# Packed 64-row decay and fifth mixing products, a regrouped order of mixing steps, and the last channel addition on GpSimd

## The chip, the cores and the metric

The kernel runs on 1 core of one Trainium2 chip. The metric is the device time of one execution in microseconds (us); lower is better. All arithmetic is in fp32. In the profile PE is TensorE's matmul stream and PEld its weight loads, DVE is VectorE, ACT is ScalarE, POOL is GpSimd, and SP is SyncE, which issues the DMAs.

## What is computed

Two layers over x of 64 sequences, 64 steps, 256 channels. The first is a transformer layer: self attention, cross attention, and an MLP (not touched). The second is a recurrent block, of which this is the part that matters:

```python
xxx = jnp.tanh((xa + sx * maa_x) @ maa_w1).reshape(b, l, 5, 32)
xxx = jnp.einsum('blfd,fde->blfe', xxx, maa_w2)          # five mixing products
xm = xa[:, :, None] + sx[:, :, None] * (maa_stack + xxx) # xk, xw, xv, xr, xg
w = jnp.exp(-jnp.exp(time_decay + jnp.tanh(xw @ td_w1) @ td_w2))
r, k, v = xr @ Wr.T, xk @ Wk.T, xv @ Wv.T
g = silu(xg @ Wg.T)
# per head: out_t = r_t (u * k_t v_t + s);  s = k_t v_t + w_t * s   (a scan over the 64 steps)
x1 = x + groupnorm(out) * g @ Wo.T
xc = layernorm(x1)                                       # channel mixing
xk2, xr2 = xc + sx2 * ffn_maa_k, xc + sx2 * ffn_maa_r
return x1 + sigmoid(xr2 @ Wfr.T) * (square(relu(xk2 @ Wfk.T)) @ Wfv.T)
```

## The kernel before

x lives in SBUF as 32 tiles of 128 rows. The attention part works through all tiles twice and ends near 480 us. `late_phase` then works in 16 runs (`RUNS`) of 256 rows (`RT`, two tiles). It is written as one instruction stream per engine; each engine runs its stream strictly in order, and semaphores tie the streams together. So the order within a stream is the schedule. `body(s, u)` is a pipeline stage of every engine: in body s the scan of run s goes on together with the mixing and projections of run s + 1, the normalisation of run s + 2, the MLP of run s + 3, the group normalisation of run s - 1 and the output projection and residual of run s - 2. Bodies -2 to 3 are written out, 4 to 11 are a hardware loop, 12 to 15 are written out again.

Names that the change and the prediction's steps touch:

- **PE.** `mix_pair` (L1031) makes mixing products 0 to 3, in pairs, from 32-row tiles of weights; even-numbered steps go to PSUM bank `even` (bank 4) and odd ones to `odd` (bank 5). `mix_last` (L1042) makes the fifth product into `even` from a 128-row weight tile, half of whose rows are zero: `maa_w2b[:, c]` holds the real weights only in rows 64c onward (the other tile's 64 rows are zero), so the four 128x128 matmuls contract over 128 rows to use 64. `decay` (L1082) makes `td_w2` products into bank `small` (bank 3) in the same way. `project` (L1071, and L1052 for the decay's first product) makes the projections NW, NV, NK, NR, NG; `up` (L982) and `down` (L991) are the MLP; `sum_heads` (L1109) reduces the read states; `project_out` (L1142) is the output product of run s - 2. An fp32 matmul shows as two records, so "x8" is four matmuls.
- **DVE.** A run's scan is 8 groups. Group n is `key_values` (L1749), `scan` (L1763) and `read` (L1774; for groups 2 and 3 POOL reads, L901). Between the groups stand, by hand, `mix` (L1729, two halves a step), `add_heads` (L1791), `add_residual` (L1826, adds run s - 2's output product to x), `centre` (L1795, L1802), `sum_squares` (L1812), `mlp_residual` (L1697) and others. Steps 0 and 1 of `mix` stand after group 3's read, step 2 in n == 4, step 3 in n == 5, step 4 in n == 6.
- **POOL.** `mix` (L892) adds xa to each mixed product; step m is called at n = m + 3. `add_mlp_bias` (L868), `scale` (L909, group normalisation, after all groups), `step_back` (L875), `make_bonus` (L884).
- **ACT.** `decay` (L1425) takes the exponential of the decay products; `make_decays` (L1433) that of its negative, for the next run's scan.
- **Channel mixing.** Its 16 runs (`ch_` functions) start in the last three bodies (`early(s)`: s = 13, 14, 15, two runs a body) and go on alone after them. On DVE `ch_mix` (L1867) makes two inputs, `ch_finish` multiplies tanh + 1 by the value product (L1875) and then adds half of that to x (L1879). `ch_shift` (L938) is on POOL; `ch_transpose`, `ch_keys` (L1251), `ch_receptances` (L1266) and `ch_values` (L1281) on PE. In n == 2 of these bodies DVE's order is `add_heads`, `ch_mix` (which waits for POOL's `ch_shift`), `mlp_moments`, `add_residual`. PE's `mix_pair(s + 1, 0)` waits for `add_residual(s - 2)`, since `project_out` wrote bank `odd`:

```python
if m == 0:
    pe.wait_ge(mixer_tanh, r + 1)
    ...
    if later(r - 2):
        pe.wait_ge(x_ready, r - 2)
```

SP stores run s when `ch_out_ready` reaches s + 1.

## Time and profile before

| | |
|---|---|
| median of 3 runs | 1130.16 us (1126.83 to 1130.65) |
| the profiled execution | 1127.48 us, span 1125.7 us |
| mean granted TensorE clock | 0.988 |
| busy over the span | PE 95%, DVE 81%, ACT 63%, POOL 53% |
| attention part | to about 480 us |
| bodies of the late phase | 480 to 1050 us, one full one about 33.7 us |
| channel mixing alone | 1050 us to the end |

The span is that of the instructions on the core; 1.8 us of the execution's time lie around it. The median of the three runs is 2.7 us over the profiled execution. A share of the whole span says little here: the stages have different limits, so each is read by itself.

### The profile page before, as it was taken

How to read it: one execution, taken by the hardware profiler on the slowest of the kernel's cores; microseconds unless marked ns; L12 is line 12 of the kernel's file. 1: busy time of each engine (PE TensorE's matmuls, PEld its weight loads, DVE VectorE, ACT ScalarE, POOL GpSimd, SP SyncE). 2: the span in 40 equal slices, each digit the busy share in tenths (PEclk: the TensorE clock that was granted, in tenths of full speed). 3: DMA queues.
4: the chain of work that ended last, by engine and by line, in shares of the span. 5: the costliest groups of instructions: out<-in, count | busy, mean ns of one | idle time of the engine just before them, and what ended most of it. 6: DMA issues, size and time to landing. Idle time of an engine off the chain costs nothing.

```text
span 1125.7 us, 34405 instructions
## 1 busy us (share of the span) xinstructions
PE 1067.1 (95%) x12992; PEld 898.8 (80%) x12992; DVE 914.3 (81%) x1677; ACT 705.7 (63%) x1606; POOL 591.5 (53%) x520
## 2 busy tenths in 40 slices
PE   5899999999999998999999999999999997887798
PEld 4889889888988987778778888778888776665677
DVE  5987777888777775129999999999999999899864
ACT  4778788777877875555545565546555545535574
POOL 4787878878788784034443444443444343433121
PEclk9999999999999998999999999999999999889999
DMA  9500000011111110022233332133332123304011
GB/s 331 167 4 2 0 0 3 3 40 47 44 37 46 38 38 2 1 59 68 54 75 85 85 85 60 35 75 84 84 84 61 34 74 85 84 2 120 20 38 57
DMA packets 39868, 65.01 MB, mean 58 GB/s; under 512 B 4385, under 2 KB 26209, under 8 KB 39393
## 3 DMA queue, kind: packets, MB, share of 16 engines
q1 hardware_dynamic: 39776, 63.75, 21.3%
q8 instruction: 62, 1.02, 0.4%
q14 instruction: 30, 0.24, 0.1%
HBM read 55.35 MB, written 8.39 MB: 57 GB/s over the span
## 4 chain that ended last, share of the span: by engine, by line
PE 83%; DVE 9%; issue 4%; ACT 3%; POOL 1%; DMA 0%; DVEq 0%; ACTq 0%; POOLq 0%
PE psum L982 10%; PE psum L353 10%; PE psum L991 9%; PE psum L1071 9%; PE psum L267 5%; PE psum L336 5%; PE psum L368 5%; PE psum L297 4%; PE psum L280 3%; PE psum L1031 3%; PE psum L1109 2%; PE psum L1251 2%; PE psum L310 2%; PE psum L1142 2%; DVE shared L1763 2%
## 5 line engine op out<-in xcount | busy, mean ns | idle before, releaser
L1763 DVE TENSOR_TENSOR_SCAN shared<-late_wT,shared 128x512 f32<-128x512 f32 x128 | 175.6, 1372 | 0.0
L892 POOL TENSOR_TENSOR late_xm<-late_mixed,late_xa 128x512 f32<-128x512 f32 x64 | 91.4, 1438 | 106.2 <-DVE late_mixed L1729 106.1
L232 POOL TENSOR_TENSOR shared<-shared,att_row_max 128x512 f32<-128x512 f32 x128 | 132.5, 1054 | 17.3 <-DVE att_row_max L564 17.3
L353 PE MATMUL psum<-shared 128*128 128x128 f32 x1024 | 126.7, 277 | 0.0
L453 ACT ACTIVATE shared<-shared 128x512 f32<-128x512 f32 x128 | 80.5, 631 | 67.5 <-POOL shared L232 67.4
L982 PE MATMUL psum<-late_glnT,w 128*128 128x256 f32 x512 | 119.8, 387 | 1.8 <-ACT late_glnT L1359 1.8
L353 PEld LDWEIGHTS psum<-shared 128*128 128x128 f32 x1024 | 121.0, 194 | 0.2 <-ACT shared L462 0.2
L564 DVE TENSOR_REDUCE att_row_max<-shared 128x8 f32<-128x512 f32 x128 | 86.8, 679 | 41.0 <-POOL shared L225 40.9
L991 PE MATMUL psum<-w,late_hT 128*128 128x256 f32 x512 | 118.6, 380 | 1.0 <-ACT late_hT L1368 0.9
L901 POOL TENSOR_TENSOR shared<-shared,late_rT 128x512 f32<-128x512 f32 x32 | 40.8, 1274 | 143.0 <-DVE shared L1763 143.0
L982 PEld LDWEIGHTS psum<-late_glnT,w 128*128 128x128 f32 x512 | 95.8, 192 | 18.0 <-issue 2.8
L991 PEld LDWEIGHTS psum<-w,late_hT 128*128 128x128 f32 x512 | 93.6, 190 | 12.6 <-ACT late_hT L1368 1.8
L225 POOL TENSOR_TENSOR shared<-shared 128x512 f32<-128x512 f32 x64 | 80.1, 1273 | 39.8 <-DVE shared L557 38.2
L225 POOL TENSOR_TENSOR shared<-shared,self_bias 128x512 f32<-128x512 f32 x64 | 80.2, 1277 | 31.0 <-DVE shared L557 31.0
L1368 ACT ACTIVATE late_hT<-psum,cols 128x256 f32<-128x256 f32 x128 | 53.8, 471 | 65.7 <-PE psum L982 65.3
L1749 DVE TENSOR_TENSOR shared<-shared,psum 128x504 f32<-128x504 f32 x128 | 85.5, 669 | 11.2 <-ACT shared L1412 11.0
L267 PEld LDWEIGHTS psum<-shared 64*64 64x64 f32 x4096 | 66.3, 136 | 21.3 <-issue 21.2
L1729 DVE SCALAR_TENSOR_TENSOR late_mixed<-psum,cols,late_sx 128x256 f32<-128x256 f32 x160 | 67.9, 474 | 14.3 <-PE psum L1031 9.4
L462 ACT ACTIVATE shared<-psum 128x512 f32<-128x512 f32 x128 | 68.5, 586 | 9.1 <-PE psum L280 9.1
L267 PE MATMUL psum<-shared 64*64 64x17 f32 x4096 | 72.7, 209 | 0.0
L336 PE MATMUL psum<-shared 128*128 128x128 f32 x512 | 69.5, 280 | 1.5 <-issue 1.5
L424 ACT ACTIVATE shared<-psum,cols 128x256 f32<-128x256 f32 x128 | 65.4, 565 | 8.1 <-PE psum L310 5.3
(167 smaller groups left out, 2433.7 us busy)
## 6 DMA issues: line engine op xcount, KB each, us to landing
shared<-v_rows SPq DMA_DIRECT2D x64, 512.0 KB, 7.3
shared<-in_enc SPq DMA_DIRECT2D x64, 128.0 KB, 2.6
v_rows<-shared SPq DMA_DIRECT2D x64, 64.0 KB, 1.8
out<-x SPq DMA_DIRECT2D x16, 256.0 KB, 2.0
x<-in_x SPq DMA_DIRECT2D x7, 512.0 KB, 9.8
w<-in_w SPq DMA_DIRECT2D x2, 1024.0 KB, 17.3
shared<-in_cross_mask SPq DMA_DIRECT2D x1, 1024.0 KB, 12.3
shared<-in_w_qkv SPq DMA_DIRECT2D x1, 768.0 KB, 4.8
```

What stands on the lines that cost most here:

```text
L225: nc.gpsimd.tensor_tensor(zs, zs, bias.unsqueeze(1).to_broadcast([P, PAIRS, S]), ALU.add).then_inc(biased, 1)
L232: nc.gpsimd.tensor_tensor(zs, zs, peak.unsqueeze(2).to_broadcast([P, PAIRS, S]), ALU.subtract).then_inc(shifted, 1)
L267: last = nc.tensor.matmul(out_banks[e ^ b][rows, pair * 32:pair * 32 + HD + 1], zT[keys, pair, rows], values[keys, u, e ^ b, pair, :], sta ...
L336: last = nc.tensor.matmul(vv[:, e * P:(e + 1) * P].rearrange("p (r d) -> p r d", d=HD), KV[k][:, u % 2, kb, e * S:e * S + P], wv[:, kb, v0 ...
L353: last = nc.tensor.matmul(dst[:, half * P:(half + 1) * P], w[:, kb, c0 + half * P:c0 + (half + 1) * P], src[:, u % 2, kb, 0:P], start=(kb ...
L564: nc.vector.tensor_reduce(out=row_max[:, u % 2, half * PAIRS:(half + 1) * PAIRS], in_=z[:, u % 2, half, :].rearrange("p (h k) -> p h k", k=S),
L892: nc.gpsimd.tensor_tensor(xm[m % XM].rearrange("p h (b t) -> p (h b) t", t=S), mixed[:, m % 2, :, :].rearrange("p h (b t) -> p (h b) t", t=S),
L982: last = nc.tensor.matmul(bank[:, (h % 2) * RT:(h % 2 + 1) * RT], w["w1"][:, kb, h * P:(h + 1) * P], glnT[:, kb, :], start=(kb == 0), stop ...
L991: last = nc.tensor.matmul(mlp[:, c * C:(c + 1) * C], hT[:, h, c * P:(c + 1) * P], w["w2"][:, h, :], start=(h == 0), stop=(h == HIDDEN - 1))
L1071: last = nc.tensor.matmul(bank[:, half * RT:(half + 1) * RT], w[name][:, kb, half * P:(half + 1) * P], xm[m % XM][:, kb, :], start=(kb == ...
L1749: nc.vector.tensor_tensor(st[:, n, :, :, 1:S], v_rep[:, n // PER_SUM, n % PER_SUM * JG:(n % PER_SUM + 1) * JG, :].rearrange("p j (b t) -> ...
L1763: nc.vector.tensor_tensor_scan(states, wT[:, u, half, :, :, :].rearrange("p j b t -> p (j b t)"), states, 0.0, ALU.mult, ALU.add).then_inc ...
```

## The change

It has four parts.

1. `decay` and `mix_last` on PE contract over 64 rows: each of the two tiles c uses its own row half (rows 64c to 64c + 63) of weights and input, and the two write different banks. The decay products now lie in `small` (c = 0) and in the upper half of `odd` (c = 1); the fifth mixing product lies in the lower halves of `even` and `odd`. ACT's `decay` and DVE's `mix(4)` read them with patterns over two banks.
2. Since `odd` holds mixing product 3 until DVE has read it, PE's `mix_last` waits for `mix(3)` instead of `mix(2)`, and `decay` stands behind `mix_last` instead of ahead of `down(s + 3, 0)`. DVE's `mix(3)` stands right behind `mix(2)` in n == 4, `mix(4)` moves from n == 6 to n == 5, and `mix(4)` waits for ACT's `decay` as well.
3. The addition to x of channel mixing moves from DVE (L1879) to POOL (`ch_add`) for 15 of 16 runs; the factor 0.5 moves into ACT's `Square` (scale sqrt(0.5) on its input).
4. In the last three bodies `add_residual(s - 2)` stands ahead of `ch_mix` in n == 2.

```diff
@@ -737,6 +737,8 @@
 
         small, even, odd, proj, o_bank, mlp = (core.banks[i] for i in (3, 4, 5, 2, 0, 1))
         k_bank, r_bank = core.banks[6:8]
+        decays = core.psum[:, 3 * 512:3 * 512 + 2 * 1280].rearrange("p (c n) -> p c n", c=CH)[:, :, 0:RT]
+        fifth = core.psum[:, 4 * 512:6 * 512].rearrange("p (c n) -> p c n", c=CH)[:, :, 0:RT]
 
         ch_xn = core.shared[:, 8192:9216].rearrange("p (a b c) -> p a b c", b=2, c=256)
         ch_xc = core.shared[:, 9216:10256].rearrange("p (a b c d) -> p a b c d", b=2, c=4, d=65)
@@ -915,6 +917,8 @@
                     step_back(s + 1)
                 if there(s):
                     make_bonus(s, u)
+                if early(s - 1):
+                    ch_add(early_run(s - 1, 1), 1)
                 for n in range(GROUPS_R):
                     if n == 5 and there(s + 3):
                         add_mlp_bias(s + 3)
@@ -926,6 +930,8 @@
                         mix(s + 1, n - 3)
                     if n == 3 and early(s):
                         ch_shift(early_run(s, 1), 1)
+                    if n == 6 and early(s):
+                        ch_add(early_run(s, 0), 0)
                 if there(s - 1) and not s_is(s, RUNS - 1):
                     scale(s - 1)
                 if s_is(s, RUNS - 1):
@@ -940,18 +946,29 @@
                                         ch_xc[:, u, :, :, 1:S + 1].rearrange("p h b t -> p (h b) t"),
                                         ALU.subtract).then_inc(ch_sx_ready, 1)
 
+            def ch_add(r, u):
+                pool.wait_ge(ch_rv_ready, r + 1)
+                xs = core.x[:, ds(r, CH * C)]
+                nc.gpsimd.tensor_tensor(xs, ch_rr[:, u, :], xs, ALU.add).then_inc(ch_out_ready, 1)
+
             def channel(s, u):
                 if there(s + 2):
                     ch_shift(s + 2, u)
+                if there(s + 1):
+                    ch_add(s, u)
 
             add_mlp_bias(0)
             bodies(pool, body)
             ch_shift(EARLY + 1, 1)
+            ch_add(EARLY - 1, 1)
             ch_shift(EARLY + 2, 0)
             scale(RUNS - 2)
             scale(RUNS - 1)
+            ch_add(EARLY, 0)
             ch_shift(EARLY + 3, 1)
+            ch_add(EARLY + 1, 1)
             ch_shift(EARLY + 4, 0)
+            ch_add(EARLY + 2, 0)
             channel(EARLY + 3, 1)
             channel_runs(pool, channel)
 
@@ -1035,12 +1052,13 @@
                             last.then_inc(mix_ready, 1)
 
             def mix_last(r):
-                pe.wait_ge(mixed_ready, r * NMIX + NMIX - 2)
-                for half in range(HALVES):
-                    for c in range(CH):
-                        a = half * RT + c * P
-                        last = nc.tensor.matmul(even[:, a:a + P], core.maa_w2b[:, c, half * P:(half + 1) * P],
-                                                mixer_b[:, :], start=True, stop=True)
+                pe.wait_ge(mixed_ready, r * NMIX + NMIX - 1)
+                for half in range(HALVES):
+                    for c, bank in enumerate((even, odd)):
+                        rows = slice(c * DD, (c + 1) * DD)
+                        last = nc.tensor.matmul(bank[:, half * P:(half + 1) * P],
+                                                core.maa_w2b[rows, c, half * P:(half + 1) * P],
+                                                mixer_b[rows, :], start=True, stop=True)
                 last.then_inc(mix_ready, 1)
 
             def project(r, m):
@@ -1077,10 +1095,11 @@
                 if later(r - 1):
                     pe.wait_ge(centred_ready, r - 1)
                 for half in range(HALVES):
-                    for c in range(CH):
-                        a = half * RT + c * P
-                        last = nc.tensor.matmul(small[:, a:a + P], core.td_w2[:, c, half * P:(half + 1) * P],
-                                                decay_in[:, :], start=True, stop=True)
+                    for c, bank in enumerate((small, odd)):
+                        rows = slice(c * DD, (c + 1) * DD)
+                        a = c * RT + half * P
+                        last = nc.tensor.matmul(bank[:, a:a + P], core.td_w2[rows, c, half * P:(half + 1) * P],
+                                                decay_in[rows, :], start=True, stop=True)
                 last.then_inc(decay_ready, 1)
 
             def bonus_sums(r):
@@ -1190,11 +1209,11 @@
                     ch_receptances(early_run(s, 0), 0)
                 if mixing:
                     project(s + 1, NV)
-                    decay(s + 1)
                 if mlp_run:
                     down(s + 3, 0)
                 if mixing:
                     mix_last(s + 1)
+                    decay(s + 1)
                 if early(s):
                     ch_values(early_run(s, 0), 0)
                 if mlp_run:
@@ -1422,9 +1441,9 @@
             def decay(r):
                 act.wait_ge(decay_ready, r + 1)
                 for half in range(HALVES):
-                    last = nc.scalar.activation(decay_exp[:, half * RB:(half + 1) * RB, :].rearrange("p b t -> p (b t)"),
-                                                small[:, half * RT:(half + 1) * RT], ACT.Exp,
-                                                bias=col(core, "time_decay", half))
+                    last = nc.scalar.activation(
+                        decay_exp[:, half * RB:(half + 1) * RB, :].rearrange("p (c b) t -> p c (b t)", c=CH),
+                        decays[:, :, half * P:(half + 1) * P], ACT.Exp, bias=col(core, "time_decay", half))
                 last.then_inc(decay_expd, 1)
 
             def make_decays(r, u):
@@ -1524,7 +1543,7 @@
                     act.wait_ge(up_ready, RUNS * UPS)
                 if later(r - 1):
                     act.wait_ge(ch_value_ready, r - 1)
-                nc.scalar.activation(ch_kk[:, u, :], ch_relu[:, :], ACT.Square).then_inc(ch_kk_ready, 1)
+                nc.scalar.activation(ch_kk[:, u, :], ch_relu[:, :], ACT.Square, scale=0.5 ** 0.5).then_inc(ch_kk_ready, 1)
 
             def ch_tanh(r, u):
                 act.wait_ge(ch_recept_ready, r + 1)
@@ -1725,11 +1744,17 @@
                 dve.wait_ge(mix_ready, r * NMIX + m + 1)
                 if later(r) or m >= 2:
                     dve.wait_ge(xm_ready, r * NMIX + m - 1)
-                for half in range(HALVES):
+                if m == NMIX - 1:
+                    dve.wait_ge(decay_expd, r + 1)
+                for half in range(HALVES):
+                    if m == NMIX - 1:
+                        products = fifth[:, :, half * P:(half + 1) * P]
+                    else:
+                        products = (even, odd)[m % 2][:, half * RT:(half + 1) * RT].rearrange("p (c t) -> p c t", c=CH)
                     last = nc.vector.scalar_tensor_tensor(
-                        out=mixed[:, m % 2, half, :], in0=(even, odd)[m % 2][:, half * RT:(half + 1) * RT],
+                        out=mixed[:, m % 2, half, :].rearrange("p (c t) -> p c t", c=CH), in0=products,
                         scalar=col(core, "maa_stack", MIX[m] * HALVES + half),
-                        in1=sx[:, half, :, :].rearrange("p b t -> p (b t)"), op0=ALU.add, op1=ALU.mult)
+                        in1=sx[:, half, :, :].rearrange("p (c b) t -> p c (b t)", c=CH), op0=ALU.add, op1=ALU.mult)
                 last.then_inc(mixed_ready, 1)
 
             def gate(r, u):
@@ -1874,10 +1899,11 @@
                 dve.wait_ge(ch_rr_ready, r + 1)
                 nc.vector.scalar_tensor_tensor(out=ch_rr[:, u, :], in0=ch_rr[:, u, :], scalar=1.0, in1=ch_bank("value", r),
                                                op0=ALU.add, op1=ALU.mult).then_inc(ch_rv_ready, 1)
-                dve.wait_ge(ch_rv_ready, r + 1)
-                xs = core.x[:, ds(r, CH * C)]
-                nc.vector.scalar_tensor_tensor(out=xs, in0=ch_rr[:, u, :], scalar=0.5, in1=xs, op0=ALU.mult,
-                                               op1=ALU.add).then_inc(ch_out_ready, 1)
+                if r == RUNS - 1:
+                    dve.wait_ge(ch_rv_ready, r + 1)
+                    dve.wait_ge(ch_out_ready, r)
+                    xs = core.x[:, ds(r, CH * C)]
+                    nc.vector.tensor_tensor(xs, ch_rr[:, u, :], xs, ALU.add).then_inc(ch_out_ready, 1)
 
             def channel(s, u):
                 ch_finish(s - 1, 1 - u)
@@ -1915,10 +1941,11 @@
                         add_heads(s - 1, 1 - u)
                     if n == 2:
                         if early(s):
+                            add_residual(s - 2)
                             ch_mix(early_run(s, 0), 0)
                         if there(s + 2) and not s_is(s, -2):
                             mlp_moments(s + 2)
-                        if there(s - 2):
+                        if there(s - 2) and not early(s):
                             add_residual(s - 2)
                     if n == 3 and there(s + 1):
                         mix(s + 1, 0)
@@ -1932,17 +1959,16 @@
                             centre(s - 1, 1 - u)
                         if there(s + 1):
                             mix(s + 1, 2)
+                            mix(s + 1, 3)
                         if early(s):
                             ch_mix(early_run(s, 1), 1)
                     if n == 5:
-                        if there(s + 1):
-                            mix(s + 1, 3)
                         if early(s):
                             ch_finish(early_run(s, 0), 0)
                         if there(s - 1) and not s_is(s, RUNS - 1):
                             sum_squares(s - 1)
-                    if n == 6 and there(s + 1):
-                        mix(s + 1, 4)
+                        if there(s + 1):
+                            mix(s + 1, 4)
                     if n == 7 and s_is(s, RUNS - 1):
                         ch_mix(EARLY, 0)
```

## Rows read from the trace of the kernel before

**Rows 1.** Busy time by stretch: us, then PE, PEld, DVE, ACT, POOL busy (instructions), clock, DMA.

```profile
506.50:536.70 30.20, 30.20 (x177) 24.59 (x176) 27.09 (x43) 16.83 (x37) 14.60 (x11) 1.00 0.34 80
...
770.87:804.59 33.72, 33.72 (x210) 27.32 (x209) 32.11 (x52) 18.93 (x42) 14.76 (x12) 1.00 0.30 70
...
939.46:981.00 41.54, 32.04 (x185) 24.35 (x184) 38.13 (x62) 19.54 (x45) 16.07 (x13) 0.92 0.27 63
...
1050.00:1126.00 76.00, 65.74 (x334) 55.70 (x332) 46.37 (x97) 45.27 (x92) 12.22 (x11) 1.00 0.10 39
```

**Rows 2.** The chain that ended last, one loop body: start us, us, what.

```profile
615.20 1.06 PE psum L1031 x8
...
621.37 0.62 PE psum L1052 x8
...
622.99 1.92 PE psum L1071 x8
624.91 0.89 PE psum L1082 x8
...
627.53 0.89 PE psum L1042 x8
...
631.88 1.73 PE psum L1071 x8
```

**Rows 3.** Timeline of another loop body: start us, us, instruction, [idle before, releaser].

```profile
787.96 2.00 DVE L1763 TENSOR_TENSOR_SCAN shared<-late_wT,shared 128x512 f32<-128x512 f32 x1
788.83 2.20 POOL L868 TENSOR_TENSOR x<-x,rows 128x512 f32 x1
...
791.98 0.87 DVE L1729 SCALAR_TENSOR_TENSOR late_mixed<-psum,cols,late_sx 128x256 f32<-128x256 f32 x2
...
792.77 0.67 DVE L1749 TENSOR_TENSOR shared<-shared,psum 128x504 f32<-128x504 f32 x1
792.93 1.20 POOL L892 TENSOR_TENSOR shared<-late_mixed,late_xa 128x512 f32<-128x512 f32 x1 [1.91 <-DVE late_mixed L1729]
...
793.36 1.85 DVE L1763 TENSOR_TENSOR_SCAN shared<-late_wT,shared 128x512 f32<-128x512 f32 x1
...
795.72 0.84 ACT L1425 ACTIVATE late_decay_exp<-psum,cols 128x256 f32<-128x256 f32 x2
...
796.80 1.19 POOL L892 TENSOR_TENSOR late_xm<-late_mixed,late_xa 128x512 f32<-128x512 f32 x1 [2.67 <-DVE late_mixed L1729]
...
798.20 1.22 DVE L1763 TENSOR_TENSOR_SCAN shared<-late_wT,shared 128x512 f32<-128x512 f32 x1
...
801.01 2.03 POOL L892 TENSOR_TENSOR late_xm<-late_mixed,late_xa 128x512 f32<-128x512 f32 x1 [3.03 <-DVE late_mixed L1729]
...
803.00 1.10 POOL L909 TENSOR_TENSOR shared<-shared,late_rstd 128x512 f32<-128x512 f32 x1
...
803.13 0.68 DVE L1749 TENSOR_TENSOR shared<-shared,psum 128x504 f32<-128x504 f32 x1 [0.34 <-ACT shared L1412]
...
804.59 0.69 DVE L1697 TENSOR_TENSOR x<-psum,x 128x512 f32 x1 [0.78 <-PE psum L991]
```

**Rows 4.** Timeline of body 13, the first with channel mixing.

```profile
951.09 1.26 POOL L901 TENSOR_TENSOR shared<-shared,late_rT 128x512 f32<-128x512 f32 x1 [2.88 <-DVE shared L1763]
951.51 2.31 DVE L1867 SCALAR_TENSOR_TENSOR late_hT<-shared,cols 128x256 f32<-128x256 f32 x4
...
954.98 0.69 DVE L1826 TENSOR_TENSOR x<-psum,x 128x512 f32<-128x512 f32 x1
...
955.81 1.95 PE L1031 MATMUL psum<-late_mixer_a,maa_w2a 32*128 32x256 f32 x8 [4.96 <-DVE x L1826]
...
973.26 0.69 DVE L1875 SCALAR_TENSOR_TENSOR w<-w,psum 128x512 f32<-128x512 f32 x1 [2.14 <-PE psum L1281]
...
973.98 0.69 DVE L1879 SCALAR_TENSOR_TENSOR x<-w,x 128x512 f32<-128x512 f32 x1
```

**Rows 5.** Busy time by stretch of 2 us within body 13, columns as in rows 1.

```profile
956.00:958.00 2.00, 2.00 (x10) 1.30 (x9) 1.66 (x3) 0.00 (x0) 0.54 (x1) 0.50 0.00 0
```

## The prediction

> **What bounds the kernel now.** I read the busy time by stretch first [rows 1]. In a full loop body (33.72 us) PE is busy for all of it and DVE for 32.11 us: PE sets the period, and DVE is close behind. Body 13 is another case: 41.54 us, PE busy for 32.04, DVE for 38.13, and the granted clock averages 0.92. In body 0 (506.50 to 536.70) PE is full and DVE has 3 us left. After 1050 us PE is busy 65.74 of 76 us and DVE 46.37. The chain that ended last is PE alone through the loop bodies. So each part has to be costed where it falls: PE's time counts in the loop as long as DVE does not take over; DVE's time counts in the last three bodies.
>
> How near DVE is, the timeline shows: in one body it waits 0.34 us for k's copy and 0.78 us for the MLP [rows 3]; with the small gaps that those waits cover, it could start `mlp_residual` 1.28 us earlier (`read(7)` starts at about 802.10, two steps of 0.61 us later comes 803.31, against 804.59). That 1.28 us is all the cover that DVE's new waits have.
>
> **PE: two products at half height.** `decay` and `mix_last` take 0.89 us each [rows 2], 8 records at 0.11. The 32-row tiles of `mix_pair` run in pairs on two row groups: 8 records with 256 columns take 1.06 us, where 8 full ones take 1.73 [rows 2]. Of the 1.06, 4 x 0.216 = 0.86 is streaming and 0.20 is the change of tile shape; the full product behind tiles pays 0.19 too (1.92 against 1.73 [rows 2]). The 64-row case with 128 columns is not in the trace; nearest is L1052, 8 tiled records with 128 columns in 0.62. By that pattern both products need 8 pairs x 0.108 = 0.86, plus 0.20 going in and 0.19 coming out, as they now stand together: 1.25 against 1.78, so 0.53 us less per body. Bounds: if pairs didn't overlap at all, 1.78 + 0.39, a loss of 0.39; with no cost for the changes of shape, a gain of 0.92. I take 0.53 by the 32-row rows, since they use row groups and two banks in the same way. PE alone would then have a period of 33.2 us.
>
> The Trainium skill (TensorEngine Tiling, Key Properties) says that a change of tiling mode drains the array. The 0.19 to 0.20 us in the rows agree; a rule of "up to 2x" without it would give 0.89.
>
> **PE's new waits.** `mix_last` now needs `mix(3)`. DVE would end it about 1.6 us after 791.98 [rows 3], at 793.6; PE comes to it at about 795.0, behind `down(s + 3, 0)`. Hidden, with 1.4 us of cover. `decay` ends about 2 us later than before, near 796.2 (795.0 + 1.25), so ACT starts L1425 near 796.3 instead of 795.72 [rows 3] and ends at 797.2. Behind it wait `make_decays` (needed only in the next body) and the normalisation of run s + 2, which has some 0.7 us of cover: nothing. The ACT form over two banks has the same count of elements: no cost, between -0.1 and +0.1.
>
> **DVE and POOL: the order of the mixing steps.** No DVE instruction is added, so its own work stays at 32.4 us. But scans and POOL's operations on SBUF exclude each other. `scan(5)` is issued at 793.36 under POOL's `mix(2)` (792.93, 1.20) and takes 1.85 instead of 1.22; POOL's `mix(4)`, issued at 801.01 just behind `scan(7)`, takes 2.03; and L868, issued at 788.83 while a scan from 787.96 was already waiting, let that scan go first [rows 3]. So: whoever asked first. POOL's `mix(3)` and `scan(6)` are apart now (796.80, 798.20: 1.19 and 1.22 [rows 3]). After the change, counted from `mix(2)`'s start M = 791.98:
> - `mix(3)` ends at M + 1.6, `key_values(6)` runs to M + 2.2, and only then does `scan(5)` ask. POOL's `mix(2)` runs from M + 0.95 to M + 2.15 and its `mix(3)` is ready behind it, so POOL goes on first, narrowly, to M + 3.27. `scan(5)` ends at M + 4.4. Before, it ended at M + 3.23 but with `mix(3)` (0.79) still to do: a loss of 0.4.
> - `sum_squares`, then `mix(4)` from M + 6.0 to M + 6.9 (`decay`'s exponential is there at M + 5.2, no wait); POOL's `mix(4)` runs M + 6.95 to M + 8.14; `scan(6)`, issued at M + 7.38, waits 0.7.
> - `scale` (1.10 us, L909 [rows 3]) now comes behind `mix(4)`, lets `scan(6)` go first and holds up `scan(7)` by 0.45 (before, it ran at 803.00 beside no scan).
> - What `mix(4)` itself held up is POOL's, not DVE's. Rounding taken in, `read(7)` is 1.3 us later than before.
>
> The cover is 1.28. DVE's period becomes 33.7 us: it takes over exactly where PE was, and PE's 0.53 us is not seen in bodies 2 to 12. Bounds of the port waits: none of them gives 32.45 (PE's 33.2 binds); each of the three operations holding up a scan for its whole length (1.2 + 1.2 + 1.1 against 0.7 now) gives +2.8, less 1.28: +1.5 per body.
>
> **Bodies -1, 0 and 1.** DVE has more than 1.3 us left, so PE's gain counts: 3 x 0.53 = 1.6 us.
>
> **Bodies 13 to 15.** In body 13 `ch_mix` is issued at 951.51 but POOL's L901 holds SBUF until 952.35; then it takes its four steps, and `add_residual` comes at 954.98. PE waits 4.96 us for it, and its next product runs at 0.50 of the clock: 1.95 us for 8 records instead of 1.13 [rows 4, 5]. So `add_residual` (0.69) fits into the hole ahead of `ch_mix`: free, and PE starts `mix_pair` 3.5 us earlier, at the full clock (the 2.4 GHz level). DVE then loses two small waits for `mix_pair` and, above all, the 2.14 us ahead of `ch_finish` [rows 4]. Moving L1879 away saves 0.61 from start to start, twice a body. Against that: POOL's additions (1.26 us, the price of L901, same shape [rows 4]; nothing to 2.0 if a scan is in front) hold up `scan(1)` after the first `ch_finish` by 0.65, so there nothing is won; the other lies beside `sum_squares` and `mix(4)`. The regrouped mixing costs its 1.3 again, partly within these waits, and part of `ch_mix` of the second run meets POOL's `mix(3)`. Sum: body 13 -2.3, body 14 (the same three waits stand there again, at 994 to 1015 us) -2.1, body 15, with no mixing, about 0: -4.4 us. Bounds: DVE's gaps of 3.4 and 3.8 us and six L1879 all gone, -10.9; the port taking nearly all, -1.
>
> **After 1050 us.** PE is the bound (keys, values, receptance, transposition: 5.6 us a run against DVE's 3). POOL is busy 12 of 76 us [rows 1] and takes nine more additions of 1.3 us beside idle time; the order ch_shift, ch_add puts each addition some 2 us ahead of the next shift's data. The last run's addition stays on DVE, and the store behind it too. The factor in `Square` is free. 0, between -1 and +1.
>
> The Trainium skill (GPSIMD Engine Reference, Engine selection) advises against additions on GpSimd, as about twice as slow: 1.26 against 0.69 us agrees. By it alone the tail would lose if POOL were on its chain; there it is idle for 64 of 76 us [rows 1].
>
> **Sum.** 1127.5 - 1.6 - 0 - 4.4 = 1121.5 us on the profiled execution, which ran 2.7 us under the median of the three runs; the same -6.0 on the median is 1124.2. I give **1123**, 1.5 over the sum, half the distance to the median; the rivals' times have the same 1.5. About 0.5% (5.6 us) is what a measurement of this kernel can tell from no change, so the forecast lies just at that line.
>
> **Rivals.**
> - *The scan goes first (0.25).* POOL's lead at M + 2.15 is under 0.1 us. If `scan(5)` gets in ahead of `mix(3)`, it ends 0.7 us earlier than now, `mix(4)` waits some 0.25 for the exponential, the rest is as above: DVE's period 33.0, PE's 33.2 binds, and 11 bodies give another 5.8: 1121.5 - 5.8 + 1.5 = 1117.
> - *The port takes more than the cover (0.15): slower.* Place: `scan(5)`, `scan(6)`, `scan(7)` of bodies 2 to 14. It decides once their waits together pass the present ones by more than 1.28 + 0.5 us a body. With half the upper bound, 0.75 x 11 = 8.3, and bodies 13 and 14 winning 1.5 less: 1121.5 + 9.8 + 1.5 = 1132.8. For it: three POOL operations are moved next to scans; against: the rows show turns being taken. The Trainium skill (SBUF — State Buffer, two separate sides) has the pair of ports as an exclusive lock, held for the whole instruction by whoever starts first. By it the cost of each meeting is what is left of the operation, as counted.
> - *The tiles don't overlap (0.07).* PE's period rises by 0.39: 14 x 0.39 - 4.4 on the profiled execution gives 1128.6 + 1.5 = 1130. It would contradict the 32-row rows.
> - *The clock falls all the same (0.08).* PE now runs ahead in bodies 13 and 14 and waits about 3 us ahead of the second key product. If the clock falls there, half of the 4.4 is lost: 1125.
>
> **Range and chances.** The forecast (0.45) by itself holds 1119 to 1127. 1113 to 1132 takes in the second case and most of the third. Faster by over 0.5%: half of the forecast and the first rival, 0.48; slower by over 0.5%: part of the port case, 0.12; within: 0.40.
>
> **What would show it.** The chain in the loop turns from PE to DVE, the period stays within 0.1 of 33.7 (33.2 for the first rival, above 34.1 for the second). L1082 and L1042 together take 1.25 us. `scan(5)` takes 2.2 us, `scan(6)` 1.9. PE's 4.96 us is gone and the clock is 1.00 in bodies 13 and 14. If the periods of bodies 13 and 14 don't fall by about 2 us each, the forecast is wrong in its main term.

## The result, and the profile after

The changed kernel takes **1120.26 us** (median of 4 runs, 1118.13 to 1122.14), and the kernel before 1130.22 us on the same chip: ratio 0.9918 (0.9889 to 0.9947), 9.3 us less by the ratio and 10.0 between the two medians. A second series gave 1118.04 us and 0.9911 (0.9889 to 0.9932), by the ratio 10.0 us less. Gains below are by the ratio. The forecast was 1123 us. The profiled execution took 1118.86 us, 8.6 less than that of before.

The page of the changed kernel, busy time and the chain that ended last by engine, and below them the chain of the kernel before:

```profile
PE 1061.3 (95%) x12992; PEld 883.5 (79%) x12992; DVE 916.1 (82%) x1662; ACT 702.6 (63%) x1606; POOL 608.1 (54%) x535
PE 60%; DVE 27%; issue 7%; ACT 3%; DVEq 1%; DMA 1%; SPq 0%; POOL 0%; ACTq 0%; POOLq 0%
...
PE 83%; DVE 9%; issue 4%; ACT 3%; POOL 1%; DMA 0%; DVEq 0%; ACTq 0%; POOLq 0%
```

The first line hardly differs from that of before. The chain does: DVE's share went from 9% to 27% of the span, and in the loop bodies the chain now runs through DVE's instructions. The busy time by stretch of the changed kernel (columns as in [rows 1]; one full body stands for the loop, the fourth and fifth stretch begin inside bodies 14 and 15):

```profile
505.97:535.64 29.67, 29.67 (x177) 23.69 (x176) 27.41 (x43) 16.80 (x37) 13.67 (x11) 1.00 0.34 78
768.04:801.49 33.45, 33.41 (x209) 26.27 (x208) 32.95 (x52) 18.69 (x42) 14.80 (x12) 1.00 0.31 72
936.73:977.26 40.53, 31.49 (x200) 23.76 (x199) 39.25 (x64) 20.89 (x47) 15.75 (x14) 1.00 0.33 77
977.26:1014.00 36.74, 30.88 (x187) 23.62 (x186) 35.34 (x54) 18.00 (x39) 17.60 (x14) 0.95 0.27 63
1014.00:1041.00 27.00, 22.47 (x123) 16.82 (x122) 26.33 (x36) 12.54 (x28) 11.24 (x8) 0.94 0.15 53
1041.00:1117.00 76.00, 66.94 (x332) 56.41 (x330) 38.52 (x87) 45.24 (x92) 24.59 (x21) 0.97 0.10 39
```

Body 0 took 30.18 us before; the loop body took 33.72. In body 13 PE is busy for less time than before, at a clock of 1.00 instead of 0.92.

**Where the 8.6 us lie** in the two profiled executions, counted between starts of `mlp_residual` and, in the last bodies, of DVE's gate product:

| stretch | before | after | difference | predicted |
|---|---|---|---|---|
| up to body 0 | 506.51 | 505.97 | -0.54 | -0.53 |
| bodies 0 and 1 | 61.78 | 60.91 | -0.87 | -1.06 |
| bodies 2 to 11 | 337.37 | 335.11 | -2.26 | 0 |
| body 12 | 33.80 | 34.74 | **+0.94** | 0 |
| start of body 13 to body 14's gate | 51.48 | 47.53 | -3.95 | -2.3 |
| body 14's gate to body 15's | 39.26 | 36.66 | -2.60 | -2.1 |
| from there to the end | 95.5 | 96.2 | +0.7 | 0 |

The start of body 0 by itself says little: over the kernels of this study, whose attention part is the same, it lay anywhere between 503.40 and 507.15 us. Body -1 can be told apart, though: counted between starts of `mlp_residual` it took 26.59 us in the four traces with products at full height (before, e1, e2, e4) and 26.09 us in the ten with tiles. So 0.50 of the first row's 0.54 us is the tiles'.

The rows of bodies 12 and 13 have to be read together. The start of `mlp_residual` is a marker on DVE, and DVE comes to it later now in body 13, but has less to do behind it. The timeline of the kernel before, then that of the changed one, at the start of body 13:

```profile
940.65 1.89 DVE L1763 TENSOR_TENSOR_SCAN shared<-late_wT,shared 128x512 f32<-128x512 f32 x1
942.47 1.19 DVE L1855 SCALAR_TENSOR_TENSOR neg_mean<-neg_mean,rstd 128x20 f32<-128x20 f32 x1
...
937.92 1.22 DVE L1788 TENSOR_TENSOR_SCAN shared<-late_wT,shared 128x512 f32<-128x512 f32 x1
939.05 0.16 DVE L1880 SCALAR_TENSOR_TENSOR neg_mean<-neg_mean,rstd 128x20 f32<-128x20 f32 x1
```

From the start of `mlp_residual` to DVE's gate product body 13 takes 8.55 us before and 7.26 after. From gate product to gate product body 12 takes 35.02 us before and 34.76 after, and body 13 takes 42.93 and 40.27. So body 12 lost nothing, and bodies 12 and 13 together gave 3.0 us (0.94 against 3.95 in the table).

**In the loop**, the timeline of the changed kernel, DVE's and POOL's work around the moved mixing steps, one body:

```profile
789.11 1.65 DVE L1754 SCALAR_TENSOR_TENSOR late_mixed<-psum,cols,late_sx 128x256 f32<-128x256 f32 x4
790.05 1.19 POOL L894 TENSOR_TENSOR shared<-late_mixed,late_xa 128x512 f32<-128x512 f32 x1 [1.90 <-DVE late_mixed L1754]
791.19 1.18 POOL L894 TENSOR_TENSOR late_xm<-late_mixed,late_xa 128x512 f32<-128x512 f32 x1
791.26 2.20 DVE L1788 TENSOR_TENSOR_SCAN shared<-late_wT,shared 128x512 f32<-128x512 f32 x1
793.50 0.84 ACT L1444 ACTIVATE late_decay_exp<-psum,cols 128x256 f32<-128x256 f32 x2 [0.73 <-PE psum L1101]
795.06 0.88 DVE L1754 SCALAR_TENSOR_TENSOR late_mixed<-psum,cols,late_sx 128x256 f32<-128x256 f32 x2
796.02 1.18 POOL L894 TENSOR_TENSOR late_xm<-late_mixed,late_xa 128x512 f32<-128x512 f32 x1 [3.65 <-DVE late_mixed L1754]
796.43 1.85 DVE L1788 TENSOR_TENSOR_SCAN shared<-late_wT,shared 128x512 f32<-128x512 f32 x1
797.16 2.02 POOL L911 TENSOR_TENSOR shared<-shared,late_rstd 128x512 f32<-128x512 f32 x1
798.92 1.34 DVE L1788 TENSOR_TENSOR_SCAN shared<-late_wT,shared 128x512 f32<-128x512 f32 x1
```

`scan(5)` starts in the record 0.07 us after POOL's `mix(3)`, and POOL went first: the scan takes 2.20 us instead of 1.22. `scan(6)` takes 1.85, behind POOL's `mix(4)`. `scan(7)` is held for only 0.12 us (1.34) by `scale`. ACT's exponential is done at 794.34, DVE comes to `mix(4)` at 795.06: no wait. The chain of waits of the changed kernel over the same stretch (start, us, what) lies on these very instructions:

```profile
789.11 1.65 DVE late_mixed L1754 x4
790.76 0.59 DVE shared L1774
791.34 2.12 DVE shared L1788
...
795.06 0.88 DVE late_mixed L1754 x2
...
796.53 1.77 DVE shared L1788
```

**In the last bodies**, the timeline of the changed kernel, PE's products behind waits, and the first addition on POOL with the scan beside it:

```profile
948.94 1.13 PE L1048 MATMUL psum<-late_mixer_a,maa_w2a 32*128 32x256 f32 x8 [0.91 <-ACT late_mixer_b L1421]
967.43 1.97 PE L1270 MATMUL psum<-late_hT,WfkT 128*128 128x256 f32 x8 [2.92 <-DVE w L1900]
981.26 1.28 POOL L952 TENSOR_TENSOR x<-w,x 128x512 f32<-128x512 f32 x1 [1.95 <-DVE w L1900]
981.70 1.93 DVE L1788 TENSOR_TENSOR_SCAN shared<-late_wT,shared 128x512 f32<-128x512 f32 x1
988.60 1.13 PE L1048 MATMUL psum<-late_mixer_a,maa_w2a 32*128 32x256 f32 x8 [1.42 <-DVE x L1851]
1006.12 3.44 PE L1270 MATMUL psum<-late_hT,WfkT 128*128 128x256 f32 x8 [2.93 <-DVE w L1900]
1026.80 3.68 PE L1270 MATMUL psum<-late_hT,WfkT 128*128 128x256 f32 x8 [1.58 <-DVE late_hT L1892]
```

The wait of 4.96 us [rows 4] is down to 0.91, and `mix_pair` takes 1.13 us, not 1.95. A new wait of 2.9 us stands ahead of the second key product, and behind it the same eight records take 1.97 us in body 13 and 3.44 us in body 14.

### The profile page after: what moved, and what is told of

Same layout as the page of the kernel before. It is cut to its first block, busy times and chain, and to the rows that moved or that the text cites. A ratio compares the mean times of both kernels' runs of the same rounds, so it can differ in the third digit from the quotient of the medians.

```text
span 1117.1 us, 34410 instructions
## 1 busy us (share of the span) xinstructions
PE 1061.3 (95%) x12992; PEld 883.5 (79%) x12992; DVE 916.1 (82%) x1662; ACT 702.6 (63%) x1606; POOL 608.1 (54%) x535
## 4 chain that ended last, share of the span: by engine, by line
PE 60%; DVE 27%; issue 7%; ACT 3%; DVEq 1%; DMA 1%; SPq 0%; POOL 0%; ACTq 0%; POOLq 0%
PE psum L353 9%; DVE shared L1788 9%; PE psum L267 5%; PE psum L999 5%; PE psum L336 5%; PE psum L1008 4%; PE psum L368 4%; PE psum L1089 4%; DVE shared L1774 4%; PE psum L297 4%; PE psum L280 3%; DVE late_mixed L1754 3%; PE psum L1270 2%; PE psum L310 2%; PE psum L1300 2%
## 5 line engine op out<-in xcount | busy, mean ns | idle before, releaser
L1788 DVE TENSOR_TENSOR_SCAN shared<-late_wT,shared 128x512 f32<-128x512 f32 x128 | 192.4, 1503 | 0.0
L894 POOL TENSOR_TENSOR late_xm<-late_mixed,late_xa 128x512 f32<-128x512 f32 x64 | 79.7, 1255 | 59.9 <-DVE late_mixed L1754 56.3
```

Source lines behind the costliest of these rows:

```text
L1788: nc.vector.tensor_tensor_scan(states, wT[:, u, half, :, :, :].rearrange("p j b t -> p (j b t)"), states, 0.0, ALU.mult, ALU.add).then_inc ...
```

## The experiments

The ratio is always to the kernel before, which ran on the same chip in the same series, with its 95% interval. **Theory A** was the prediction's account; each rival stands in the text on record.

### The three parts, one at a time

**e1: the kernel before with the residual ahead of channel mixing alone.**

```diff
                         if early(s):
+                            add_residual(s - 2)
                             ch_mix(early_run(s, 0), 0)
...
-                        if there(s - 2):
+                        if there(s - 2) and not early(s):
                             add_residual(s - 2)
```

> The kernel before with the fourth part alone: add_residual ahead of ch_mix in bodies 13 to 15. Theory A (the hole in front of mix_pair and the half clock behind it are most of the gain of the last bodies): PE's waits of 4.96 and 3.66 us fall to about 1 us, body 13 gets about 2.5 us shorter and body 14 about 1.5, and the whole 3 to 5 us. The loop stays at 33.72 us a body. Theory B (DVE's own load is what bounds those bodies, and PE's hole only stands beside it): under 1.5 us.

1122.41 us, ratio 0.9962 (0.9944 to 0.998): -4.3 us. The loop body stays at 33.72 to 33.75. Gate to gate, body 13 takes 39.58 us (42.93 before) and body 14 37.28 (39.26). The timeline of this kernel has the short wait, and a product close to its full-clock length behind it, in both bodies:

```profile
949.95 1.13 PE L1031 MATMUL psum<-late_mixer_a,maa_w2a 32*128 32x256 f32 x8 [1.51 <-DVE x L1826]
989.53 1.18 PE L1031 MATMUL psum<-late_mixer_a,maa_w2a 32*128 32x256 f32 x8 [1.43 <-DVE x L1826]
```

So one moved call of 0.69 us is worth 4.3 us. Two things in this trace say how. In body 14 the clock is at 0.50 again right behind the product (from 991 to 997 us, for as long as before), and the body is 1.98 us shorter all the same: there the gain is not the clock's. And the call is nearly free on DVE: `ch_mix`, which now starts behind it, takes 1.73 us instead of 2.31 [rows 4], since POOL's L901 is all but over by then (it ends at 949.98, `ch_mix` starts at 949.72).

**e2: the kernel before with the additions on POOL alone** (the lines of part 3 of the change: `ch_add` on POOL, the factor in `Square`).

> The kernel before with the third part alone: the channel addition on GpSimd for 15 runs, factor in Square. Theory A (the second ch_finish of a body lies on DVE's path, but its addition then holds up scan(1) at the port): 0.6 us in each of bodies 13 to 15 at most, 0 to 2 us in all; scan(1) of bodies 14 and 15 takes 1.9 us instead of 1.22. Theory B (DVE's time in these bodies is worth its full price): six times 0.61 = 3.7 us. Neither expects anything of the part after the last body, where PE is the bound.

1127.98 us, ratio 0.999 (0.9973 to 1.0007): no difference that can be told from zero (-1.1 us by the ratio, +0.5 between the medians). The timeline of this kernel, body 14:

```profile
988.08 1.28 POOL L950 TENSOR_TENSOR x<-w,x 128x512 f32<-128x512 f32 x1 [1.95 <-DVE w L1890]
988.52 1.93 DVE L1778 TENSOR_TENSOR_SCAN shared<-late_wT,shared 128x512 f32<-128x512 f32 x1
```

DVE saves a step of 0.61 us and gets back a scan that is 0.71 longer (1.93 for 1.22). Body 13 takes 43.27 us, 0.34 more than before, body 14 38.64, 0.62 less.

**e3: the kernel before with the tiles and the new mixing order alone** (parts 1 and 2).

> The kernel before with the first two parts alone: 64-row tiles, decay behind mix_last, the regrouped mixing steps, mix(4) waiting for the exponential. Channel addition and residual as before. Theory A (PE's 0.53 us a body is gained, DVE's port waits take half of it back): loop body 33.5 us, 3 to 4 us by body 12, then the last bodies lose about 1 us to the port: 2 to 4 us faster in all. Theory B (the regrouping is only there to make room, the last bodies are where the change works): within 1 us of the kernel before.

1124.22 us, ratio 0.9971 (0.9954 to 0.9987): -3.3 us. Loop bodies take 33.43 to 33.58, body 12 34.74, and bodies 13 and 14 keep their holes (PE waits 4.10 and 3.67 us). The three parts sum to -4.3 - 1.1 - 3.3 = -8.7 us by the ratios, and to -7.7 by the medians, since e2's share is not distinct from zero; the whole gave -9.3 and -10.0. So they add up within what these series can tell.

### What holds the loop at 33.5 us

**e4: the changed kernel, both products at full height again, order kept.**

```diff
-                                                core.maa_w2b[rows, c, half * P:(half + 1) * P],
-                                                mixer_b[rows, :], start=True, stop=True)
+                                                core.maa_w2b[:, c, half * P:(half + 1) * P],
+                                                mixer_b[:, :], start=True, stop=True)
...
```

> The changed kernel with its matmuls of mix_last and decay at 128 rows again (zero rows of the weights back in), everything else as changed, the order and the two banks too. Theory A (tiles are worth 0.53 us of PE a body, DVE with its port waits needs 33.5): PE needs 33.7 and binds again, loop body 33.7 to 33.8 instead of 33.5, and the whole 3 to 5 us slower than the changed kernel. Theory B (DVE alone sets the loop body since the regrouping): no difference, loop body 33.5. If DVE's and PE's loads add up where both are full, it may be more than 33.8.

1122.84 us, ratio 0.996 (0.9942 to 0.9977), some 5 us slower than the changed kernel. Two starts of `mlp_residual` on its timeline, one body apart:

```profile
737.77 0.69 DVE L1716 TENSOR_TENSOR x<-psum,x 128x512 f32 x1
771.51 0.69 DVE L1716 TENSOR_TENSOR x<-psum,x 128x512 f32 x1
```

33.74 us: PE binds again at its old period, and the chain of this loop body is PE's alone. So DVE, with all of the port's waits, stays under 33.74, and the tiles do bring the 0.2 to 0.3 us a body that are seen.

**e5: the changed kernel with `centre` behind `mix(3)`.** Then POOL's `mix(2)` and `mix(3)` are over before DVE asks for `scan(5)`.

```diff
                     if n == 4:
-                        if there(s - 1) and not s_is(s, RUNS - 1):
-                            centre(s - 1, 1 - u)
                         if there(s + 1):
                             mix(s + 1, 2)
                             mix(s + 1, 3)
+                        if there(s - 1) and not s_is(s, RUNS - 1):
+                            centre(s - 1, 1 - u)
```

> The changed kernel with centre moved from ahead of mix(2) to behind mix(3) in n == 4, so that 1.4 us of DVE's work without the shared port stands between mix(3) and scan(5). Port theory (DVE binds the loop body at 33.5 us, of which scan(5) waits 1.0 us behind POOL's mix(3)): scan(5) falls from 2.2 to about 1.3 us, DVE's need drops under PE's 33.2, and the loop body becomes 33.2: 3 us less in all. Rival (33.5 is PE's own period with the tiles, or is set by the new wait of mix(4) for the exponential): the body stays at 33.5.

1116.53 us, ratio **0.9898** (0.9882 to 0.9915), the fastest kernel of the study. Loop bodies take 33.01 to 33.51, mostly 33.2. The timeline of this kernel:

```profile
789.72 1.22 DVE L1788 TENSOR_TENSOR_SCAN shared<-late_wT,shared 128x512 f32<-128x512 f32 x1
792.98 0.88 DVE L1754 SCALAR_TENSOR_TENSOR late_mixed<-psum,cols,late_sx 128x256 f32<-128x256 f32 x2 [0.37 <-ACT late_decay_exp L1444]
```

and its chain of waits, a little earlier in the same body:

```profile
790.86 0.65 PE psum L1059 x8
791.50 0.45 PE psum L1101 x8
791.95 3.65 PE psum L1008 x16
```

The scan is back at 1.22 us, `mix(4)` now waits 0.37 for the exponential, and the chain is PE's: this is what the first rival forecast, reached by another order. It also gives the tiles' price on the path, 0.65 + 0.45, and 0.19 for the product behind them: 1.29 us.

**e9: the changed kernel with `sum_squares` behind `mix(4)`**, so that POOL's `mix(4)` is over before `scan(6)`.

```diff
-                        if there(s - 1) and not s_is(s, RUNS - 1):
-                            sum_squares(s - 1)
                         if there(s + 1):
                             mix(s + 1, 4)
+                        if there(s - 1) and not s_is(s, RUNS - 1):
+                            sum_squares(s - 1)
```

> The changed kernel with sum_squares moved behind mix(4) in n == 5, so that POOL's mix(4) runs beside it instead of in front of scan(6). Port theory: scan(6) falls from 1.85 to 1.22 us; mix(4) then comes 1 us earlier and may wait 0.2 to 0.4 us for ACT's exponential; loop body 33.2 to 33.3. Rival (the wait for the exponential counts): mix(4) waits 0.5 us or more and the body stays at 33.5 or goes up.

1119.72 us, ratio 0.9935 (0.9919 to 0.9952), loop 33.46 to 33.54 (the last body 33.26): no gain over the changed kernel. Its timeline:

```profile
791.81 0.88 DVE L1754 SCALAR_TENSOR_TENSOR late_mixed<-psum,cols,late_sx 128x256 f32<-128x256 f32 x2 [0.19 <-ACT late_decay_exp L1444]
793.74 0.35 ACT L1490 ACTIVATE late_log_var<-late_moments,eps 128x66 f32<-128x66 f32 x1 [0.89 <-issue]
794.16 1.22 DVE L1788 TENSOR_TENSOR_SCAN shared<-late_wT,shared 128x512 f32<-128x512 f32 x1
794.30 1.59 PEld L1089 LDWEIGHTS psum<-shared,WkT 128*128 128x128 f32 x8 [0.26 <-DVE shared L1774]
796.19 0.42 PEld L1020 LDWEIGHTS psum<-ident,late_xn 128*128 128x128 f32 x4 [0.30 <-ACT late_xn L1400]
```

`scan(6)` did fall to 1.22 us, and `mix(4)` waits 0.19 us, both as the port theory expected; the loop body stayed at 33.5, as the rival expected, but not for the rival's reason. The chain of this body is PE's. ACT's `late_log_var` starts 0.08 us behind the end of the later `sum_squares`, the normalisation behind it in ACT's stream comes later, and PE's transposition of its result takes 0.55 us in the chain instead of e5's 0.44. The other half comes straight from DVE: the weight load of the key projection waits for `key_values`, and the projection takes 1.85 us in the chain instead of e5's 1.73. Together 0.23 us: 33.2 became 33.5. The wait went off the port and onto PE, by two ways that no expectation had.

**e7: both moves (e5 and e9) together.**

> Both moves of the last two together. Port theory: both scans at 1.22, PE binds at 33.2 us a body (PE's own sum: 33.73 less 0.53), no better than either alone if each already lets PE bind; 3 to 4 us less than the changed kernel. Rival (something besides the port keeps DVE at 33.5): as the changed kernel.

1117.93 us, ratio 0.9912 (0.9897 to 0.9927), loop 33.49 to 33.58. Both scans take 1.22 us, but `mix(4)` comes so early that it waits 1.30 us for the exponential:

```profile
794.40 0.88 DVE L1754 SCALAR_TENSOR_TENSOR late_mixed<-psum,cols,late_sx 128x256 f32<-128x256 f32 x2 [1.30 <-ACT late_decay_exp L1444]
```

The chain is PE's, with the same two products drawn out as in e9 (1.95 and 0.55 us). The expected 33.2 did not come.

### The last bodies

**e8: the changed kernel with the additions back on DVE** (part 3 undone).

> The changed kernel with the channel addition on DVE again, and the factor 0.5 in it. Theory A (the third part gives little, since each POOL addition ahead of scan(1) blocks it for 0.65 us): body 14 and 15 within 0.7 us each of the changed kernel, 0 to 2 us slower in all. Theory B (with the hole in front of mix_pair gone DVE alone bounds bodies 13 to 15, so that the addition is worth its price there): 0.6 us twice a body, 3 to 4 us slower.

1118.8 us, ratio 0.9916 (0.9895 to 0.9937), against 0.9918 and 0.9911 for the changed kernel. With e2, part 3 shows nothing that these series can tell from zero, in either surrounding. One thing in the trace of its profiled execution (1121.98 us) bears on part 4: the residual stands ahead of `ch_mix` here, PE waits only 1.43 us ahead of `mix_pair` in body 14, and the clock is at 0.50 from 991 to 1000 us all the same. That body takes 39.15 us gate to gate, where the changed kernel's takes 36.66. e4's profiled execution has the same (0.50 from 996 to 1005 us, 39.19).

**e6: the changed kernel with the residual back behind channel mixing** (part 4 undone; the diff of e1 the other way round).

> The changed kernel with add_residual behind ch_mix and mlp_moments again in bodies 13 to 15. Theory A (what the residual alone gave on the kernel before, 4.3 us, is lost): PE's hole ahead of mix_pair is 3.5 to 5 us again in bodies 13 and 14, and the kernel is 3 to 5 us slower than the changed one. Theory B (DVE, now fuller from the regrouping, bounds these bodies whatever PE does): within 2 us of the changed kernel.

1124.68 us, ratio 0.9968 (0.9954 to 0.9983): about 6 us slower than the changed kernel. The timeline of this kernel has the holes again, in bodies 13 and 14:

```profile
952.58 1.13 PE L1048 MATMUL psum<-late_mixer_a,maa_w2a 32*128 32x256 f32 x8 [4.10 <-DVE x L1851]
993.75 1.29 PE L1048 MATMUL psum<-late_mixer_a,maa_w2a 32*128 32x256 f32 x8 [3.65 <-DVE x L1851]
```

From 994 to 1002 us its granted clock averages 0.57, where the changed kernel's is 1.00.

**e10: the changed kernel with the first run's `ch_finish` right behind the second run's `ch_mix`**, to shorten the new wait of 2.9 us ahead of the keys.

```diff
                             ch_mix(early_run(s, 1), 1)
-                    if n == 5:
-                        if early(s):
                             ch_finish(early_run(s, 0), 0)
+                    if n == 5:
```

> The changed kernel with ch_finish of a body's first run right behind ch_mix of its second, at the end of n == 4, instead of behind read(5). The value product is there by then, and DVE's load is the same; only PE's wait ahead of the second key product shrinks, from 2.9 us to under 1. Clock theory (that wait is what lets the clock fall in bodies 13 and 14, and 3.44 us for eight records instead of 1.97 lies on the path): no stretch at half clock at that product, bodies 13 and 14 up to 1.5 us shorter in some executions, and the times of the runs less scattered; 1 to 4 us in all. Rival (these bodies are DVE's whatever the clock does): under 1 us.

1126.99 us, ratio 0.999 (0.9972 to 1.0009): 8 to 9 us **slower** than the changed kernel, all of its gain gone. The timeline of this kernel, body 14:

```profile
1003.91 0.69 DVE L1900 SCALAR_TENSOR_TENSOR w<-w,psum 128x512 f32<-128x512 f32 x1 [0.98 <-PE psum L1300]
1004.67 1.26 POOL L952 TENSOR_TENSOR x<-w,x 128x512 f32<-128x512 f32 x1 [2.82 <-DVE w L1900]
1005.10 1.93 DVE L1788 TENSOR_TENSOR_SCAN shared<-late_wT,shared 128x512 f32<-128x512 f32 x1
1010.20 3.65 PE L1089 MATMUL psum<-shared,WkT 128*128 128x256 f32 x8 [3.49 <-DVE shared L1774]
```

The wait ahead of the keys is short now (0.87), but DVE waits 0.98 us for the values, the addition on POOL then falls on `scan(5)`, and everything behind is later, until PE waits 3.49 us one product further on and runs at half clock after it. Two of these effects had not been counted, so the run is no clean test of the clock. Its profiled execution took 1122.40 us, 3.5 over the changed kernel's, and bodies 13 and 14 (41.49 and 39.00 us gate to gate, against 40.27 and 36.66) hold that; the median of its 12 runs is 4.6 us above that again; seven of them had a mean clock of 0.985 or less, and the one at 0.992 took 1120.45 us. How those divide between order and clock was not settled.

**e11: e5's and e10's edits together.**

> The changed kernel with centre behind mix(3) and ch_finish of the first run right behind ch_mix of the second. If the two gains are independent (port in the loop, PE's hole in the last bodies): loop body 33.2 us, and the whole 3 to 6 us under the changed kernel, the fastest of all so far. Rival: the last bodies give back what the loop gains, as the fastest so far.

1121.82 us, ratio 0.9949 (0.9931 to 0.9966): the loop runs at 33.22 to 33.25, and the last bodies give back more than it gains, with the same wait of 3.49 us ahead of the key projection.

### The same kernel again

**e12: the changed kernel, unaltered.**

> The changed kernel itself once more, with more runs, since its ratio of 0.9918 rests on four runs and its executions differ by 4 us. If the experiments add up (undoing the residual or the tiles costs 4 to 6 us, moving centre gains 2): ratio 0.990 to 0.993. If it comes out above 0.995, the losses of e4, e6 and e10 against it are smaller than they look and lie within the scatter of the last bodies' clock.

Median 1118.04 us, but the execution that was profiled took 1121.33, at a mean clock of 0.986 against 0.989. The timeline of that execution has the wait that stands at 967.43 in the first one, and another end:

```profile
968.07 3.75 PE L1270 MATMUL psum<-late_hT,WfkT 128*128 128x256 f32 x8 [2.93 <-DVE w L1900]
```

2.93 us of waiting, then 3.75 us for what took 1.97. Body 13 lasted 42.08 us gate to gate here, at a clock of 0.50 from 968 to 974 us, and 40.27 there. What one execution loses in this place is the size of the differences between parts of the change, so a statement on the last bodies needs the medians.

## Why the prediction was right, and where its sizes were off

The forecast's sign, range and mechanism held; the gain was 9.3 us instead of 6 to 7. In the two profiled executions it was 8.6 against a sum of 6.0, and nearly all of the difference is one term: bodies 2 to 11, counted at nothing, gave 2.26. Step by step:

- **The tiles: right.** 1.25 us predicted, 1.29 measured (e5), 0.49 us saved of 0.53. The change of shape costs 0.65 - 0.45 = 0.20 going in and 0.19 coming out. The third rival (no overlap) is out. The Trainium skill (TensorEngine Tiling, Key Properties) says that a change of tiling mode drains the array; the rows agree, and a plain halving would have promised 0.89.
- **PE's and ACT's new waits: right**, as long as the order is that of the change. `mix_last` and `mix(4)` wait for nothing. e7 shows how near the exponential was: with `mix(4)` some 2 us earlier it costs 1.30.
- **The port: right in kind, off by 0.2 us in size.** `scan(5)` 2.20 (2.2 predicted) and `scan(6)` 1.85 (1.9). The largest error is in the step that "`scale` ... holds up `scan(7)` by 0.45": it held it 0.12. `scale`, released at 798.28 by `scan(6)`, was done 0.90 us later and not 1.10, so only 0.26 us of it were left when `scan(7)` was requested at 798.92. The three losses were counted as 0.4, 0.7 and 0.45, which is 1.55 us, and were then taken as 1.3 without a working; with 1.55 the sum would have given a DVE period of 34.0. Measured they are 0.35, 0.63 and 0.12, or 1.10 (`read(7)` is 1.08 us later than before, counted from `mix(2)`), against a cover of 1.28. So DVE's period is 33.5 and not 33.7, and PE's gain was half seen where it was counted at zero: -2.26 us in bodies 2 to 11. e4 shows that without the tiles these bodies are back at 33.74, e5 that without the turn lost in `scan(5)` they are at 33.2. The first rival's condition was not met (POOL went first, by 0.07 us), though its size, 33.2 a body, was what e5 then gave. The second rival is out: the meetings take less than the cover. The Trainium skill (SBUF — State Buffer, two separate sides) gives the pair of ports to one engine for a whole instruction; the 2.20, 1.85 and 1.93 us are each what was left of POOL's operation (1.11, 0.77, 0.84) and then 1.08 or 1.09 us, which agrees.
- **Bodies -1, 0, 1: right** in the first two (-0.50 and -0.52 of -0.53 each), and -0.36 in body 1, at whose end DVE's wait of 0.86 us for the MLP is used up: -1.4 of -1.6 in all.
- **Body 12: right.** It was counted with the loop, at nothing. The 0.94 us in the table is the marker's: from gate product to gate product it went from 35.02 to 34.76 us.
- **Bodies 13 and 14: right in cause; the size of body 13 is open.** The forecast's main term was -2.3 and -2.1. The first profiled execution gave -2.7 and -2.6 from gate to gate, e12's, of the same kernel, -0.9 and -2.7: body 13 was 1.8 us longer at half clock. e1 has -3.35 and -1.98 from the residual alone. The charge that "the regrouped mixing costs its 1.3 again" was too high: in e3, where the regrouping stands without the residual, it moved these bodies by -0.17 and +0.42. The prediction names its terms here but doesn't add them up, so the rest can't be put down to one of them.
- **The clock: half right.** In the changed kernel's two executions it no longer falls at 956 and 996 us. But part 4 doesn't secure that: with it, the clock fell near the second of these places in e1, e4 and e8. The fourth rival had its place right too: behind the new wait of 2.9 us ahead of the keys it fell in body 14 (1006.12) and, in e12, in body 13 too. It took not "half of the 4.4": bodies 12 to 14 gave 5.6 us in the first execution and 3.9 in e12's. The +0.7 us of the tail goes with the clock as well, though no run separates the two: it took 95.5 us in the two executions whose clock stayed at 1.00 there (before and e3) and 96.2 in this one, with two stretches at 0.50 (1027 to 1030 us, 1054.5 to 1057.5).
- **Part 3: right, at nothing.** The addition holds up `scan(1)` (1.93 us) as predicted, and it brings DVE nothing on the path.

The forecast's time leaned 1.5 us towards the median of three runs; the before kernel's medians in the four series that followed were 1127.4 to 1128.0 us. So it leaned on scatter: against the median of 1120.26 the sum of 1121.5 would have missed by 1.2 us instead of 2.7. Profiled execution against profiled execution that sum missed by 2.6 (1118.86).

Three things are open. The gain of part 4 body by body can't be separated from the clock's scatter by single executions. In the direct comparison of e5 and the changed kernel the loop bodies differ by 0.2 to 0.3 us in the traces, but the intervals (0.9882 to 0.9915 and 0.9889 to 0.9932) overlap. And the share of the clock in e10 is not known.

## What to carry to other kernels

When two engines are near each other (here 33.7 and 32.4 us a body), taking 0.5 us a body from the one on the chain is worth only what the other leaves: make the sum for both. And when bodies are compared, count from a second marker too: one body seemed 0.94 us longer from one instruction and 0.26 shorter from another. A step of 0.7 us that makes another engine wait 5 us is worth more than its length (here 4.3 us for two of them): look in the trace for the longest waits of the bound engine and move up what ends them. And where two engines hold each other up at SBUF, put independent work between the requests; here POOL's operation went first by 0.07 us and a scan took 2.20 us, and with 1.4 us of other work in between it took 1.22 (e5).

## What the runs showed that was not expected

- **The same wait, two outcomes.** PE's wait of 2.92 to 2.93 us ahead of the keys was followed by the 2.4 GHz level in one execution (1.97 us for eight records) and by the 1.2 GHz level in another of the same kernel (3.75 us). A wait of 1.58 us was followed by 3.68 us for the same records (at 1026.80). In e1 and e8 the clock was at 0.50 right behind a wait of only 1.43 us. So the length of one wait does not say whether the clock falls; what else decides was not tested.
- **The scatter goes with the clock.** Of the changed kernel's ten runs the one at a mean clock of 0.984 took 1122.14 us, two at 0.986 took 1121.33 and 1121.66, two at 0.987 took 1118.58 and 1120.14, four at 0.989 took 1116.84 to 1118.86, and one at 0.994 took 1117.05.
- **An operation that had to wait at the port is quicker afterwards.** A scan alone takes 1.22 us; after POOL's operation has ended (at 792.37, 797.20 and 982.54) the waiting scan needs 1.08 or 1.09. POOL's `scale` shows the same: 2.02 us from 797.16, 0.90 of it after the scan's end at 798.28, where it takes 1.10 alone. So in these rows a meeting costs 0.13 to 0.20 us less than what is left of the other's operation.
